# Attention inside a macaron block: q and k copied whole out of PSUM, and DVE's small steps spread over other units

## The reference

```python
x = x + 0.5 * ffn(layernorm(x))      # router, top 2 of 16 experts, clamped swiglu, weighted sum
x = x + attn(layernorm(x))
x = x + 0.5 * ffn(layernorm(x))

def attn(x, W_attn, b_attn, W_proj, b_proj):        # 16 heads of 8 channels
    q, k, v = split(x @ W_attn + b_attn, 3)         # each to (batch, head, token, 8)
    att = einsum('bhqd,bhkd->bhqk', q, k) / sqrt(8) # causal mask
    y = einsum('bhqk,bhkd->bhqd', softmax(att), v)
    return y @ W_proj + b_proj
```

## Time and profile before

| | us |
|---|---|
| median of 3 runs (range) | 847.68 (847.01 to 850.09) |
| the profiled execution | 847.43 |
| its span, first to last instruction | 845.6 |
| PE busy | 517.7 (61%) |
| DVE busy | 508.3 (60%) |
| ACT busy | 314.8 (37%) |
| POOL busy | 333.4 (39%) |
| attention's first exponential | 249.42 |

### The profile page before, as it was taken

One profiled execution on the slowest core, in us unless ns is written; L12 is line 12 of the kernel. 1 busy time (PEld: TensorE's weight loads), 2 busy tenths in 40 slices (PEclk: granted clock), 3 DMA queues, 4 the chain that ended last, 5 costly groups with the idle time before them and its releaser, 6 DMA issues.

```text
span 845.6 us, 18950 instructions
## 1 busy us (share of the span) xinstructions
PE 517.7 (61%) x6235; PEld 351.5 (42%) x6235; DVE 508.3 (60%) x2562; ACT 314.8 (37%) x602; POOL 333.4 (39%) x332
## 2 busy tenths in 40 slices
PE   2304059978756969696969978453731899229400
PEld 2303048857523535353535545231420687118300
DVE  6727348847766757585857878544245687017822
ACT  1001038846324535353535534221211687017300
POOL 2774740052464343535252030516076002740274
PEclk9999979979869899898989989677655799559855
DMA  9911125535536070615152460101011355214332
GB/s 300 293 53 54 53 61 144 147 94 134 168 126 220 9 222 28 198 50 178 54 173 74 128 200 1 39 14 44 7 47 59 97 150 141 65 48 128 111 93 60
DMA packets 107230, 90.21 MB, mean 107 GB/s; under 512 B 11025, under 2 KB 99474, under 8 KB 106770
## 3 DMA queue, kind: packets, MB, share of 16 engines
q1 hardware_dynamic: 72850, 59.86, 22.9%
q0 software_dynamic: 8192, 16.79, 6.7%
q10 hardware_dynamic: 26112, 12.59, 5.1%
HBM read 47.25 MB, written 41.94 MB: 105 GB/s over the span
## 4 chain that ended last, share of the span: by engine, by line
PE 37%; issue 31%; DVE 13%; another core or an unknown queue 8%; POOL 4%; DMA 3%; ACT 2%; SPq 1%; ACTq 0%; DVEq 0%; POOLq 0%
PE banks L1501 11%; PE banks L1512 5%; PE banks L1489 4%; DVE by_token L772 3%; POOL by_token L483 3%; PE banks L1291 2%; PE banks L1241 2%; PE banks L1267 2%; PE banks L1216 1%; PE banks L1435 1%; PE banks L1269 1%; PE banks L1232 1%; DMA k_by_part<-k_parts 1%; PE banks L1197 1%
## 5 line engine op out<-in xcount | busy, mean ns | idle before, releaser
L772 DVE CUSTOM_DVE_ANT_0 by_token<-banks,konst_sb 128x128 f32<-128x128 f32 (+1 forms) x512 | 147.1, 353 | 64.0 <-remote 43.8
L533 POOL DMA_INDIRECT rows_by_expert<-by_token,posi x120 | 116.7, 973 | 103.8 <-DVE posi L958 69.3
L1501 PE MATMUL banks<-xT,pT 128*64 128x128 f32 x1536 | 119.8, 297 | 41.8 <-issue 31.8
L1501 PEld LDWEIGHTS banks<-xT,pT 128*64 128x64 f32 x1536 | 92.0, 147 | 65.0 <-issue 55.6
L605 ACT ACTIVATE pT<-banks 128x1536 f32<-128x1536 f32 x64 | 92.8, 1450 | 64.5 <-PE banks L1269 61.7
L483 POOL DMA_INDIRECT by_token<-results_by_tile,tilepos x64 | 60.9, 951 | 119.6 <-DMA results_by_tile<-ysb 100.7
L706 ACT ACTIVATE pT<-w_experts 128x384 f32 x192 | 90.0, 516 | 34.4 <-PE banks L1512 12.3
L483 POOL DMA_INDIRECT yg<-results_by_tile,tilepos x64 | 61.4, 959 | 70.7 <-DMA results_by_tile<-ysb 52.2
L1106 DVE SCALAR_TENSOR_TENSOR sig<-banks,sig 128x256 f32<-128x256 f32 x96 | 40.4, 421 | 80.9 <-ACT sig L716 67.4
L1512 PE MATMUL banks<-pT,gT 128*64 128x128 f32 x768 | 64.7, 287 | 7.4 <-issue 3.9
L716 ACT ACTIVATE sig<-banks 128x256 f32<-128x256 f32 x96 | 36.8, 384 | 69.5 <-remote 54.3
(11 more groups left out here) (160 smaller groups left out, 1033.2 us busy)
## 6 DMA issues: line engine op xcount, KB each, us to landing
xt<-rows_by_expert SPq DMA_DIRECT2D x192, 64.0 KB
results_by_tile<-ysb ACTq DMA_DIRECT2D x96, 128.0 KB
q_stack<-q_by_part SPq DMA_DIRECT2D x8, 1024.0 KB
k_stack<-k_by_part SPq DMA_DIRECT2D x8, 1024.0 KB
q_by_part<-q_parts SPq DMA_DIRECT2D x16, 384.0 KB, 3.2
k_by_part<-k_parts SPq DMA_DIRECT2D x16, 384.0 KB, 3.3
x_resident<-in_x SPq DMA_DIRECT2D x8, 256.0 KB, 5.4
w_experts<-in_w_gu SPq DMA_DIRECT2D x1, 2048.0 KB
```

What stands on the lines that cost most here:

```text
L533: pool.indirect_dma_start(out=rows_dram, out_offset=bass.IndirectOffsetOnAxis(ap=posi[:, c:c + 1], axis=0), in_=rows_of(f, q)[:, i, :], in ...
L772: last = nc.vector.tensor_tensor_reduce(masked[:, (3 * g + qt) * P:(3 * g + 2 * qt + 1) * P], of, lag, 1.0, NEG * NEG_BELOW, ALU.add, ALU. ...
L1501: last = nc.tensor.matmul(bank[2 + k % 2][h * HALF:(h + 1) * HALF, at:at + P], w_tile[:, 2 * k + i, which * F + h * HALF:which * F + (h + ...
```

## The change

The new steps of a pair's units are: unit 0 k; 1 v, k's subtraction, statistics; 2 division, aggregation; 3 normalisation and residual sum; 4 x; 5 q of the pair two ahead; 6 division and q's subtraction; 7 residual sum. ACT first copies q or k whole to SBUF (`take`), which gives bank 7 back, and then makes the first part from that copy; DVE subtracts within SBUF. For pair 1, q is projected, copied and split ahead of the units.

```diff
+            def take(which, x, at=7):
                 act.wait_ge(a_made[which], x + 1)
+                beyond_first(act, a_low[which], x)
+                nc.scalar.activation(rest[which][:, :], bank[at][:, :], ACT.Identity).then_inc(a_taken[which], 1)
+
+            def high(which, x):
+                act.wait_ge(a_taken[which], x + 1)
                 beyond_first(act, a_spread[which], x * 48)
-                nc.scalar.activation(parts[which][:, 0, :], bank[at][:, :], ACT.Identity).then_inc(a_high[which], 1)
+                nc.scalar.activation(parts[which][:, 0, :], rest[which][:, :], ACT.Identity).then_inc(a_high[which], 1)
...
                 dve.wait_ge(a_high[which], x + 1)
-                beyond_first(dve, a_low[which], x)
-                nc.vector.tensor_tensor(rest[which][:, :], bank[at][:, :], parts[which][:, 0, :], ALU.subtract).then_inc(a_rest[which], 1)
+                nc.vector.tensor_tensor(rest[which][:, :], rest[which][:, :], parts[which][:, 0, :], ALU.subtract).then_inc(a_rest[which], 1)
...
-                if steps.q is not None:
-                    split_rest(0, steps.q)
-                if steps.k is not None:
-                    split_rest(1, steps.k)
                 if steps.divide is not None:
                     divide(steps.divide)
+                if steps.q_rest is not None:
+                    split_rest(0, steps.q_rest)
+                if steps.k_rest is not None:
+                    split_rest(1, steps.k_rest)
                 if steps.combine is not None:
                     stats(steps.combine)
+                if steps.moments:
+                    moments()
...
-                for step, sem_read in ((steps.q, a_rest[0]), (steps.k, a_rest[1]), (steps.v, a_vs), (steps.x, a_xT)):
+                for step, sem_read in ((steps.q, a_taken[0]), (steps.k, a_taken[1]), (steps.v, a_vs), (steps.x, a_xT)):
...
                 for k in range(DUOS):
                     pe.wait_ge(s_ysb[k], 2 * TURNS)
-                pe.wait_ge(a_xT, 2)
+                project(0, 1)
+                pe.wait_ge(a_taken[0], 2)
                 max_T(0, 0)
...
         if v % 2 == 0:
             if j == 0:
-                self.q = pair(1)
+                self.k = pair(1)
             if j == 1:
-                self.k = pair(1)
+                self.v = self.k_rest = pair(1)
+                self.combine = pair(2)
+            if j == 2:
+                self.moments = pair(2) is not None
             if j == 3:
-                self.combine = pair(2)
+                self.normalise = pair(2)
         else:
             if j == 0:
-                self.v, self.normalise = pair(1), pair(2)
+                self.x = pair(2)
             if j == 1:
-                self.x = pair(2)
+                self.q = pair(2)
+            if j == 2:
+                self.q_rest = pair(2)
```

More of the change, by code:

```diff
@@ L236, in build_block @@
         spare = sb("spare", [P, 1])
+        spare3 = sb("spare3", [P, 1])
         gu_last = by_token[:, 0:E * 2 * F]
@@ L332, in build_block @@
         a_made = [sem(f"a_{n}_made") for n in "qk"]
+        a_taken = [sem(f"a_{n}_taken") for n in "qk"]
         a_high = [sem(f"a_{n}_high") for n in "qk"]
@@ L508, in root_of_pair, with parts_of @@
                 nc.gpsimd.tensor_tensor(a_rs[:, :], a_ve[:, :], neghalf[:, 0:QUAD], ALU.pow).then_inc(a_rstd, 1)
-            def parts_of_pair(x):
-                for which in range(2):
-                    pool.wait_ge(a_rest[which], x + 1)
-                    nc.gpsimd.tensor_copy(parts[which][:, 1, :], rest[which][:, :]).then_inc(a_mid, 1)
-                    pool.wait_ge(a_mid, x * 2 + (which - 1))
-                    nc.gpsimd.tensor_tensor(parts[which][:, 2, :], rest[which][:, :], parts[which][:, 1, :],
-                                            ALU.subtract).then_inc(a_low[which], 1)
+            def parts_of(which, x):
+                pool.wait_ge(a_rest[which], x + 1)
+                nc.gpsimd.tensor_copy(parts[which][:, 1, :], rest[which][:, :]).then_inc(a_mid, 1)
+                pool.wait_ge(a_mid, x * 2 + (which - 1))
+                nc.gpsimd.tensor_tensor(parts[which][:, 2, :], rest[which][:, :], parts[which][:, 1, :],
+                                        ALU.subtract).then_inc(a_low[which], 1)
             for f in range(2):
@@ L557, in _ @@
                     combine(2)
+                    parts_of(0, 1)
                     for x in range(1, B // 2):
-                        parts_of_pair(x)
+                        parts_of(1, x)
                         if x + 1 < B // 2:
@@ L564, in _ @@
                             combine(x + 2)
+                        if x + 1 < B // 2:
+                            parts_of(0, x + 1)
                 else:
@@ L623, in first_pair @@
                 if (t, k) == (TURNS - 1, 0):
-                    high(0, 0, 4)
+                    take(0, 0, 4)
+                    high(0, 0)
                 if (t, k) == (TURNS - 1, 1):
-                    high(1, 0, 5)
+                    take(1, 0, 5)
+                    high(1, 0)
                 if (t, k) == (TURNS - 1, 3):
@@ L641, in unit @@
                 if steps.q is not None:
+                    take(0, steps.q)
                     high(0, steps.q)
                 if steps.k is not None:
+                    take(1, steps.k)
                     high(1, steps.k)
@@ L653, in units @@
             def units():
+                take(0, 1)
+                high(0, 1)
                 evac_max(0, 0)
@@ L737, in stats, with moments @@
                 dve.wait_ge(a_comb, x + 1)
-                ch.mark(nc.vector.memset(spare[:, :], 0.0))
+                ch.mark(nc.vector.memset(spare3[:, :], 0.0))
                 for i in range(QUAD):
                     ch.mark(nc.vector.bn_stats(a_st6[:, i, :], row(x, i)))
+            def moments():
                 settle()
@@ L755, in normalise, with split_rest @@
                 last.then_inc(a_xn, 1)
-            def split_rest(which, x, at=7):
+            def split_rest(which, x):
                 dve.wait_ge(a_high[which], x + 1)
-                beyond_first(dve, a_low[which], x)
-                nc.vector.tensor_tensor(rest[which][:, :], bank[at][:, :], parts[which][:, 0, :], ALU.subtract).then_inc(a_rest[which], 1)
+                nc.vector.tensor_tensor(rest[which][:, :], rest[which][:, :], parts[which][:, 0, :], ALU.subtract).then_inc(a_rest[which], 1)
             def row_max(t, s):
@@ L795, in parts_of_first @@
             def parts_of_first(which):
-                split_rest(which, 0, 4 + which)
+                split_rest(which, 0)
                 dve.wait_ge(a_rest[which], 1)
@@ L846, in units @@
                 row_max(0, 1)
+                split_rest(0, 1)
                 attention_units(unit)
@@ L1541, in __init__ @@
         self.q = self.k = self.v = self.x = self.sums = self.project = None
+        self.q_rest = self.k_rest = self.moments = None
         self.divide = self.add = self.combine = self.normalise = None
```

6 lines of the change are left out of this document (3 added, 3 removed).

## The result

The changed kernel takes 841.43 us (839.06 to 842.43, 6 runs), the kernel before beside it 848.53 (847.01 to 850.09, 6 runs): a ratio of 0.991, 95% interval 0.989 to 0.993. The profiled execution has a span of 837.1 us, 8.5 less than before. The forecast of 835 was 6 us too low, and the gain that carried 11 of its 12.5 us did not come: the pairs with gathers gave 0.65 us together. In the experiments one execution of e2_no_gather took 1041.25 us where the other three took 818.59 to 822.65; the median and the ratio given for it go by those three.

A forecast was written before the change was run, and what follows sets the result against it. Gathers were taken to cost 9.15 us in each of five pairs, with TensorE and VectorE near their limits elsewhere. Gains of 11 + 0.6 + 1.5 - 0.6 = 12.5 us off 847.43 gave 835, range 824 to 846.

The forecast's parts named there:

- Bank waits: TensorE's waits for q's and k's subtraction before bank 7 is reused: 4.5 and 3.6 us, to disappear.
- First gather: GpSimd's first gather in a pair: to stand 11.7 us after exponential 0 instead of 16.0.
- The burst sooner against a fixed pattern of silence: Gathers start 4.31 us earlier with unchanged silence after them: a gather pair gains 2.2 us, five of them 11.
- one moment at 8.56: Within the silence, TensorE's updates get through once, 8.56 us after the first gather; placed at the weights of unit 4.
- such a pair still takes over 40: Sign of a wrong forecast: a pair with a gather still over 40 us, where 38.6 was expected.
- rival (b): Gather pairs: the gather costs what it did and VectorE is the bound; 4.8 us gained, 842.6 us, chance 0.23.
- Pair without gathers: The attention pair in which GpSimd gathers nothing: to gain 0.6 us.
- routing pair: Next pair, where routing of the second half fills VectorE: 1.7 us gain at most, 1.5 taken.
- start: Start of attention, where q of pair 1 is projected ahead: to lose 0.6 us, within 0 to 3.2.
- Pair 7 and the rest: Last attention pair and the work behind it: no gain forecast, 0 us.
- Rival (c): Earlier gathers share the DMA engines with q's and k's stacks, silence still ends at 317.7: slower, 858 us, chance 0.08.
- Rival (d): GpSimd's combine meets q's subtraction in unit 6 and holds it 1.28 us: 841 us, chance 0.04.

The follow-up runs named there:

- e2_no_gather: Changed kernel without the eight gathers a pair between the attention units (output wrong): 821.06 us, ratio 0.962 to the kernel before.
- e1: Kernel before with only the copy and split of q and k in SBUF, old order of steps: 852.54 us against 852.77, ratio 0.999.
- e3: Changed kernel with the eight gathers held back until the exponential of unit 4: 848.81 us against 852.77 for the kernel before, ratio 0.995.
- e6b: Changed kernel with plain transfers of the same size instead of indirect gathers (wrong rows): 798.61 us against 848.37 for the kernel before, ratio 0.942.
- e4: Changed kernel with one more exponential waited for before every second gather, giving portions of four, two and two: 831.43 us, ratio 0.975 to the kernel before.
- r_after: Changed kernel unaltered, run again where the kernel before took about 655 us: 656.72 us, ratio 1.003 to the kernel before.

## Why the prediction was right in its number and wrong in its main step

- **Bank waits.** Right: gone, 4.5 and 3.6 us. Right too that they alone bring next to nothing, since VectorE is late next; e1 shows it, 0.999 for the whole and 16.56 for 16.76 us in units 0 to 3.
- **First gather.** Forecast 11.7 us after exponential 0, measured 11.51.
- **The burst sooner against a fixed pattern of silence: the step that failed.** "Silence then from 304.72, the moment at 310.46, the end at 313.41" took one moment at 8.56 us after the first gather, seen on TensorE in one order of the program, for a property of the burst. The end of the silence is that regular (11.45, 11.51 and 11.65 in three orders), what TensorE gets through inside it is not: 8.56 before, 4.27 after, nothing in e3. ScalarE's rows of the trace before had shown other moments, 3.48 and 7.11 us after the first gather:

```profile
309.69 0.60 ACT L593 ACTIVATE by_token<-banks 128x512 f32<-128x512 f32 x1 [1.31 <-remote]
...
313.32 0.60 ACT L612 ACTIVATE ysum<-banks 128x512 f32<-128x512 f32 x1 [3.03 <-remote]
```

  Counted from exponential 0, the weights' second half was to start at 20.3 us and exponential 4 at 23.2. The second half started at 22.96, ran at half clock, and exponential 4 stood at 24.57, 1.3 later than forecast. The next unit then took 4.79 and not 4.10, because TensorE had half clock until 318 to 319, through most of its work of that unit: 0.7 more. Forecast 38.6 a pair, measured 40.8. The forecast had named this as a sign of being wrong ("such a pair still takes over 40").
- **Why starting it sooner could not gain.** A burst costs the length of its silence less what TensorE does from what it already has, and both are nearly alike wherever the eight stand: 9.2 a pair at 16.0 us in the kernel before, 9.9 at 11.5 in the changed one and 9.95 at 17.6 (e3). The 0.78 that the changed order gains without gathers is lost again in that 0.7. A part of each figure is not silence but half clock behind it: of 9.8 in the pair shown, 8.67 lie in the long interval and 1.13 in the next (4.79 instead of 3.66). The step confused moving a cost with shrinking it. The forecast's own rival (b), "the gather costs what it did", had this at 0.23 and gave 842.6; its total too is near the measured one only with pair 7. Its second half, "DVE is the bound", holds in the units in front of the gathers (e1) and not for the distance of the two kinds of pair, in which VectorE does the same work.
- **Pair without gathers, routing pair, start.** 0.78 for 0.6; 1.26 for 1.5; -1.04 for -0.6. Sizes only.
- **Pair 7 and the rest.** Nothing was forecast, 5.17 and 1.68 came, and that is what brought the total near the forecast: luck. Pair 7 can't be put down to the steps of the change. Five traces have the changed order there, with the scatters in bursts of 16 and the silence. Two took 68.2 to 68.3 us (the changed kernel, e6b), three 74.4 to 74.8 (e2, e3, e4); the old order took 74.1 (e1), 73.45 and 71.83 (the kernel before). Between e3 and the changed kernel pair 7 differs by 6.5 us, and their ratios, 0.995 and 0.991, by some 3.4 us; so pair 7 alone can be why e3 seems slower. The changed kernel and e3 differ in TensorE's release after the first scatter:

```profile
548.84 0.28 PE L1256 MATMUL banks<-mT,select 64*128 64x128 bf16 x1 [9.67 <-remote]
```

```profile
557.07 0.28 PE L1257 MATMUL banks<-mT,select 64*128 64x128 bf16 x1 [13.90 <-remote]
```

  That is 15.71 us after the first scatter (533.13) in one and 22.92 (534.15) in the other. Which moment an update gets through at seems to hang on small shifts; that is a guess, and what sets them was not found.
- **Rival (c)**, data colliding with the stacks, did not occur: the silence ended 11.45 us after the first issue. **Rival (d)** did not occur in this comparison: GpSimd's combination (313.83 to 318.44) stood where VectorE was idle until 318.53. Without the silence it did occur, in r_after, where the combination meets q's subtraction in unit 6 (1.04 instead of 0.68 us); and the same held VectorE up in e2 and e6b.

## What to carry to other kernels

A cost that sits at a fixed delay behind an event is not made smaller by moving the event. First take the event away and see whether the cost goes with it; then cut it in portions that the other engines can work through. Portions of four instead of eight and sixteen indirect transfers gave 3%, where moving the eight gave 0.65 us in five pairs, less than 0.1%. A regularity read at one place of one trace, such as "one moment at 8.56", should enter a sum with both ends of what it could be, after a look at the same stretch on every engine that waits in it. And a change should be timed beside its predecessor again at another time: here its sign depends on a condition that neither kernel controls.

## What the runs showed of the hardware

- While GpSimd issues indirect transfers (1.26 us apart), updates that TensorE sets reach ScalarE, VectorE and TensorE itself late. For eight transfers TensorE's last release came 11.45 to 11.65 us after the first issue, for sixteen up to 22.9. Other releases came in between (in the changed kernel at 3.52, 4.27, 5.69 and 7.13 us), at moments that differ from order to order. Plain transfers of the same bytes from the same engine did nothing of the kind (e6b).
- This was so in seven of the twelve runs above and in the first comparison. In the other five no trace has it, and the kernel before takes 655 us instead of 848 to 853. The gathers' own durations are alike in both (0.94 to 1.05 us). What decides between the two was not found.
- The granted clock of TensorE was 0.50 from 309 to 318 us in a gather pair of the changed kernel, after idle times of 2.27 and 6.12, and 1.00 over a whole gather pair where there was no silence (r_after, e6b).
- GpSimd's elementwise work on SBUF stretched VectorE's cast of 8 numbers from 0.17 to 0.74, 0.77, 1.05 and 1.25 us; in these four cases the cast ended 0.02 to 0.03 us after GpSimd's operation did. Four normalising operations went from 1.17 to 3.14 and q's subtraction from 0.68 to 1.04.
